# A mixing stage of a twelve-layer decoder kernel: norms one tile further in its head, the branch product ahead of the context product, the next streams behind the branch copy

## The reference, cut to what matters

```python
x_norm = x * jax.lax.rsqrt(jnp.mean(x * x, axis=-1, keepdims=True) + RMS_EPS)
H_res_logits = (x_norm @ W_res.T).reshape(B, T, n, n) + H_res_base
H_pre_logits = x_norm @ W_pre.T + H_pre_base
H_post_logits = x_norm @ W_post.T + H_post_base
H_res = sinkhorn_log(H_res_logits)
...
H_res = (1.0 - g) * I + g * H_res
x_streams = x.reshape(B, T, n, C)
x_pre = jnp.einsum('btnc,btn->btc', x_streams, H_pre)
y = x_pre @ W_branch
x_mixed = jnp.einsum('btij,btjc->btic', H_res, x_streams)
y_distributed = jnp.einsum('btc,btn->btnc', y, H_post)
return (x_mixed + y_distributed).reshape(B, T, nC)
...
x = x + _L2_ffn_ref(_layernorm(x, axis=-1), ...)
```

## Time and profile before

| | us |
|---|---|
| median of three runs | 4217.38 (4216.12 to 4219.28) |
| the profiled execution | 4217.35 |
| its span, first to last instruction | 4215.4 |
| PE busy in it | 3910.7 (93%) |
| DVE busy | 2173.2 (52%) |
| ACT busy | 1425.1 (34%) |
| POOL busy | 313.7 (7%) |
| mean granted TensorE clock | 0.965 of full speed |

### The profile page before, as it was taken

How to read it: one execution, slowest core, us unless ns; L and a number is a source line. 1 busy time by engine, 2 the same in 40 slices (tenths; PEclk the granted TensorE clock), 3 DMA queues, 4 the chain that set the end, 5 groups by cost and what they waited for, 6 DMA issues and landing times. The chain is left out here.

```text
span 4215.4 us, 50580 instructions
## 1 busy us (share of the span) xinstructions
PE 3910.7 (93%) x18762; PEld 2088.9 (50%) x18762; DVE 2173.2 (52%) x3802; ACT 1425.1 (34%) x2570; POOL 313.7 (7%) x288
## 2 busy tenths in 40 slices
PE   8788989998989999998999889699999999999997
PEld 3333334554455555554447654355555455555554
DVE  0887765552247333333547548766556455444443
ACT  3777745553223211111113334222111133222332
POOL 1011001211001100000000111000000000000000
PEclk9899999999989999999999989899999999999998
DMA  5111121111100432311001022100010021111100
GB/s 187 45 40 35 53 76 33 33 31 58 40 33 16 178 113 103 116 54 73 1 13 55 1 101 58 64 21 21 21 40 21 1 67 36 36 35 40 65 6 23
DMA packets 133945, 215.20 MB, mean 51 GB/s; under 512 B 42576, under 2 KB 95056, under 8 KB 123104
## 3 DMA queue, kind: packets, MB, share of 16 engines
q1 hardware_dynamic: 133728, 212.19, 14.5%
HBM read 168.12 MB, written 44.04 MB: 50 GB/s over the span
## 5 line engine op out<-in xcount | busy, mean ns | idle before, releaser
L930 PE MATMUL l3a_po<-l3a_wo,l3a_cT 128*128 128x512 f32 x512 | 230.5, 603 | 3.5 <-ACT l3a_cT L1067 3.2
L436 PE MATMUL l1x_pj<-kvT,l1x_wq 128*128 128x512 f32 x512 | 228.3, 599 | 0.7 <-ACT kvT L240 0.7
L481 PE MATMUL l1x_po<-l1x_wo,l1x_cT 128*128 128x512 f32 x512 | 226.3, 596 | 1.2 <-issue 1.2
L819 PE MATMUL l3x_pj<-kvT,l3x_wq 128*128 128x512 f32 x512 | 225.5, 593 | 0.0
L819 PE MATMUL l3a_pj<-kvT,l3a_wq 128*128 128x512 f32 x512 | 224.9, 592 | 0.0
L577 DVE TENSOR_TENSOR x<-x,l1x_po 128x512 f32<-128x512 f32 x64 | 43.9, 687 | 267.1 <-PE l1x_po L481 267.1
L930 PEld LDWEIGHTS l3a_po<-l3a_wo,l3a_cT 128*128 128x128 f32 x512 | 95.5, 191 | 121.6 <-issue 110.9
L819 PEld LDWEIGHTS l3a_pj<-kvT,l3a_wq 128*128 128x128 f32 x512 | 95.5, 190 | 111.5 <-issue 111.4
L481 PEld LDWEIGHTS l1x_po<-l1x_wo,l1x_cT 128*128 128x128 f32 x512 | 95.7, 192 | 111.0 <-issue 111.0
L819 PEld LDWEIGHTS l3x_pj<-kvT,l3x_wq 128*128 128x128 f32 x512 | 95.5, 190 | 111.4 <-issue 111.4
L436 PEld LDWEIGHTS l1x_pj<-kvT,l1x_wq 128*128 128x128 f32 x512 | 94.6, 190 | 110.2 <-issue 107.2
(11 more groups left out here) (532 smaller groups left out, 7633.7 us busy)
## 6 DMA issues: line engine op xcount, KB each, us to landing
l1x_kb<-l1x_keys SPq DMA_DIRECT2D x32, 512.0 KB, 4.7
l1x_vb<-l1x_values SPq DMA_DIRECT2D x32, 512.0 KB, 3.5
l1x_keys<-l0a_kv SPq DMA_DIRECT2D x40, 256.0 KB, 2.0
fill_wk<-in_L_xattn_Wk SPq DMA_DIRECT2D x8, 1024.0 KB, 5.7
kvT<-in_L_xattn_Wv SPq DMA_DIRECT2D x8, 1024.0 KB, 5.7
l1x_values<-l0a_kv SPq DMA_DIRECT2D x32, 256.0 KB, 2.3
l1x_wq<-in_L_xattn_Wq SPq DMA_DIRECT2D x8, 1024.0 KB, 5.0
l1x_sbias<-in_L_xattn_bias SPq DMA_DIRECT2D x8, 1024.0 KB, 6.8
```

The source lines that it names most:

```text
L436: mm = pe.matmul(pj[:, j, :], wq[:, u, k, h * DH:(h + 1) * DH], m.kvT[:, k, 1, 512 * j:512 * (j + 1)], start=k == 0, stop=k == KC - 1)
L481: mm = pe.matmul(po[:, t % 2, :], cT[:, u, h, t * P:(t + 1) * P], wo[:, u, h, :], start=h == 0, stop=h == GH - 1)
L819: mm = pe.matmul(pj[:, j, :], wq[:, u, k, h * DH:(h + 1) * DH], m.kvT[:, k, 1, 512 * j:512 * (j + 1)], start=k == 0, stop=k == KC - 1)
L930: mm = pe.matmul(outs[t % 2][:, :], cT[:, h, t * P:(t + 1) * P], wo[:, u, h, :], start=h == 0, stop=h == GH - 1)
```

## The change

Head: ScalarE norms tile n+1 ahead of its wait for the product of tile n-1, and copies behind it. Mixing block: TensorE computes the branch product of tile n ahead of the tile's unit; ScalarE writes the streams of tile n+1 right behind the copy of tile n's transposed sum, waiting only for the tile that used the buffer before.

```diff
@@ head, ScalarE
                 def body(n, u):
                     if not last(n):
+                        f.norm(act, n + 1)
                         act.wait_ge(l_ready, n + 1)
-                        f.act(act, n + 1, 1 - u)
+                        f.copy(act, n + 1, 1 - u)
@@ mixing block, ScalarE
+                def streams(n):
+                    if n >= 2:
+                        act.wait_ge(mixed, n)
+                    nc.scalar.activation(xs[:, n % 2, :], m.x[:, n, :], ACT.Identity, bias=f.shift[:, n:n + 1],
+                                         scale=f.rstd[:, n:n + 1]).then_inc(xs_ready, 1)
+
+                streams(0)
                 for n in range(T):
-                    u = n % 2
-                    act.wait_ge(mixed, n if u else n + 1)
-                    nc.scalar.activation(xs[:, u, :], m.x[:, n, :], ACT.Identity, bias=f.shift[:, n:n + 1],
-                                         scale=f.rstd[:, n:n + 1]).then_inc(xs_ready, 1)
                     act.wait_ge(pre_turned, n + 2)
                     act.wait_ge(y_ready, n + 1)
                     nc.scalar.copy(preT[:, :], f.pt[:, 0:P]).then_inc(preT_ready, 1)
+                    if n + 1 < T:
+                        streams(n + 1)
                     if n >= 2:
                         norm(n - 2)
@@ mixing block, TensorE
                     pe.wait_ge(pre_ready, n + 2)
                     pe.transpose(f.pt[:, 0:P], pre[:, :], m.ident[:, :]).then_inc(pre_turned, 1)
-                    for q in later(n):
-                        unit(pe, q)
                     pe.wait_ge(preT_ready, n + 2)
                     pe.wait_ge(mixed, n + 1)
                     pe.matmul(py[:, 0:CW], preT[:, :], wb[:, :], start=True, stop=True).then_inc(y_ready, 1)
+                    for q in later(n):
+                        unit(pe, q)
                     if n >= 2:
                         turn(n - 2)
```

## The result

| | before | changed |
|---|---|---|
| median of nine runs, us | 4216.63 (4215.48 to 4219.28) | 4204.84 (4203.36 to 4207.09) |
| the profiled execution | 4217.35 | 4204.84 |
| its span | 4215.4 | 4202.9 |
| mean granted clock | 0.965 | 0.966 |

The ratio on record is 0.9975, with a 95% interval of 0.9967 to 0.9983 (the quotient of the two medians is 0.9972): faster, by 11.8 us between the medians and by 12.5 between the two profiled spans. The forecast was 4204.0.

The account below looks back on a forecast made before the run. TensorE was taken to bound the whole kernel, but not the head or, under VectorE, the mixing block. Head 6.8, mixing tiles 5.7 and tail 0.8 sum to 13.3 us, from 4217.35 to 4204.0; range 4198.5 to 4208.5.

Parts of the forecast that it names:

- The head, 6.8: In the head: last logits read at about 2486.0 where it was 2492.81, a gain of 6.8 us; lower bound 5.8.
- The two rings: In the head, per tile: TensorE's transposes and product take 2.65 us, the ring through ScalarE 2.51; TensorE's is longer.
- The loop's register work at nothing: In the head: ScalarE's loop register instructions, now behind its copy, cost nothing; uncovered, 1.0 us in all.
- The mixing tiles, 5.7: Mixing block: VectorE no longer stops, tile 7's pre sum 55.49 behind tile 0's for 61.20; gain 5.7 us, lower bound 5.1.
- The tail, 0.8: Last pre sum to the mixing block's end: 1.2 gained or 0.5 lost by the clock, weighed to 0.8 us gained.
- The middle block as long as before: Sinkhorn block, 2493 to 2632 us: left alone by the change; a length change over 2 us would count as wrong.
- The rival of the clock: In the head: TensorE, busy nearly without a gap, gets a higher clock; 5.5 us more gained, 4198.5; chance 12%.
- The loads: Behind the head: late weights start the Sinkhorn block 4 us later than forecast, hiding head gain; 4208.0; chance 12%.
- TensorE binding the mixing block: Mixing block at the low clock: TensorE needs 9.5 us a tile against VectorE's 8.07; 4221.4, slower than before; chance 3%.

Follow-up runs that it names:

- product_only: Kernel before with only TensorE's order in the mixing block changed, branch product ahead of the unit, streams where they were: 4225.14 to 4214.58 us, ratio 1.0024.
- after_b: The changed kernel measured again, on one chip with its two halves, against the kernel before: 4206.34 to 4216.64 us, ratio 0.9975.
- the runs of the parts: Head's edit alone and both mixing edits alone, each against the kernel before, on two chips: ratios 0.9988 and 0.9982 (head), 0.9995 and 0.9988 (mixing).
- head_filler: Changed kernel plus one unused 512-column matmul a tile in the head, between transposes and product: 4204.41 us against 4215.86 for the kernel before, ratio 0.9973.
- later14: Changed kernel with five more units moved from the Sinkhorn block to the mixing block: 4194.86 us against 4215.86 for the kernel before, ratio 0.9951.
- tail_turn_first: Changed kernel with five more units moved, unused wide matmuls in the head, last tile's unit behind tile 5's transposes: 4193.80 us against 4217.57 before, ratio 0.9946.

## Why the prediction was right, by its own steps

- **The head, 6.8.** Measured 6.84 at the last logits, 2485.97 for "about 2486.0". The mechanism was right, the norm off the product's path, but the hit to the hundredth is luck: 0.19 of the 6.84 is that the head was entered earlier, the transposes of tile 1, which I had said would not move, came 0.26 later for their load (2465.33 for 2465.07), and the period was 2.60 on average for my 2.65.
- **The two rings.** I had TensorE bind, at 0.91 and 1.74. But the next transposes start 1.65 after the product (2471.48 to 2473.13), so its cycle is 2.56. The ring through ScalarE, which I had at 2.51, is copy to norm 0.48, norm to transposes 0.87, transposes to copy 1.20: 2.55. Where the hardware loop jumps back, copy to norm is 0.61, and the ring 2.69 (2469.09 to 2471.78); there TensorE's weight load stands 0.15 for the norm. So neither ring clearly bounds the other.
- **The loop's register work at nothing.** It costs 0.12 to 0.13 at each of two jumps back, within the lower bound of 1.0 for all.
- **The mixing tiles, 5.7.** Measured 5.3. Tile 0 took 7.17 for 7.07. Tile 2 took 8.43 for 8.07: VectorE stands 0.30 with no releaser ahead of its addition (2648.11). Before, a stop of 0.30 at that place was put down to the product, and tile 6, from which I took the 8.07, has none. The stop is in product_only too, and tile 2 is 8.43 or 8.44 in all ten profiles with the streams moved; what causes it is open. I had the streams in place 2 us into the tile and they are there at 3.0 (2625.56 to 2628.54), still well ahead of the next pre sum at 7.17.
- **The tail, 0.8.** Measured 0.9, and this is a weighed mean that happened to be met: I had 1.2 gained or 0.5 lost, by the clock. The 16 matmuls took 7.03, as at the high level, and the last transposes 1.12 at the low one. In after_b, with the same instructions, the tail is 16.4, a loss of 0.4.
- **The middle block as long as before.** 1.0 shorter, by the clock at its start; the runs of the parts show that it is not the change's.
- **What the sum left out** is the time behind the block: 0.84 us lost at its first 16 matmuls, 2.1 lost and 1.4 regained much later, 1.5 in all. The three terms measured 6.65 + 5.3 + 0.9 = 12.8; the 0.2 gained ahead of the head and the 1.0 in the middle block, not in the sum either, nearly cancel the 1.5. That the total comes so near to 13.3 is partly chance.
- **The rival of the clock** fell. Its own argument was density, and with TensorE busy 4.96 of 5.00 us in the middle of the head the clock stayed at 0.50. head_filler shows what else could have gone wrong with it: the clock up, and the head as long. **The loads** fell: POOL's row at 2482.64, and no DMA ahead of the first unit. **TensorE binding the mixing block** fell: its mean clock did drop, to 0.83, and VectorE waited for no product. In later14, with two units in six of the tiles, they are still 8.06, though at a mean clock of 0.93 and so not under this rival's condition.
- **The two mixing edits** were priced as one, from rows and waits in which the two stops stand side by side, and nothing in the prediction says that the product's move needs the streams'. The sum was near only because both were made.

## What to carry to other kernels

When an instruction is moved forward on one engine, write down what it pushes back, and then go to the engine that consumes that: if its list has the consumer ahead of something urgent, the wait only changes its name. Here, in the tiles, one of two edits alone took 4.2 us off, the other put 7.7 on, and both together took 5.3 off. A stage in which two blocks have different bounds has work to trade: five units moved from the block that TensorE bound to the one that VectorE bound gave nearly as much again as the change. And the engine that looked idle, ScalarE at 34%, held the order in two of the misses, product_only and tail_turn_first.

## What the hardware did that I had not expected

- TensorE stayed at the lower clock through the whole head of 25 us, for ten of them busy without a gap (9.94 of 10.00), in transposes and 24-column products; with one matmul of 512 columns a tile it was at the higher from about 2473.
- A jump of ScalarE's hardware loop costs 0.12 to 0.13 us between a copy and the norm behind it (0.61 for 0.48).
- VectorE's products of 128 by 128 with two inputs go from 0.29 to 0.9, and up to 1.29 in later14, beside a product of 128 by 512 on POOL; a Sinkhorn lap of 16.6 us becomes 18.0 to 19.3.
- How long the clock stays low at the start of the next stage differs by up to 3 us between profiles, 3.0 to 6.0. With the old order it was within 3.1 to 3.4 four times; why, is open.
